# First attention of a two-block metaformer on one core: relative position terms packed per head parity, 24 products per window instead of 48, from masked queries

## The chip, the cores and the metric

The kernel runs on one core of one Trainium2 chip. The metric is the device time of one execution in microseconds (us), as the median of a few runs. TensorE is PE in the rows (its weight loads are PEld), VectorE is DVE, ScalarE is ACT, GpSimd is POOL and SyncE is SP.

## The reference, cut to what matters

Four images of 64x64 pixels and 128 channels pass through attention, a gated feed-forward layer, a second attention and a graph layer with a mixture of experts. The change is in the first attention, `_L0_conv_ref`:

```python
q = (x @ w_q).reshape(B, hh, BLOCK, ww, BLOCK, NUM_HEADS, kd)     # windows of 8x8 queries, 8 heads of 16
...
rel_w = _rel_to_abs(jnp.einsum('bghwd,dr->bghwr', pos_q, pos_emb_w))
rel_h = _rel_to_abs(jnp.einsum('bgwhd,dr->bgwhr', q_t, pos_emb_h))
return rel_h[..., :, None] + rel_w[..., None, :]
...
scores = jnp.einsum('bnhwqd,bnhwkd->bnhwqk', attn_q, key)         # 64 queries x 144 keys per window and head
attn = jax.nn.softmax(scores + pos, axis=-1)
out = jnp.einsum('bnhwqk,bnhwkv->bnhwqv', attn, value)
```

Every query has 12 numbers for the row of a key (`rel_h`) and 12 for its column (`rel_w`), and a key's position term is the sum of one of each. Each image has 64 windows, in 8 strips of 8.

## The kernel before

Each engine has its own program, written out by hand in order; semaphores tie them together, and nothing reorders them. `image(b)` runs for the four images one after the other, and the first attention (`l0conv_pe`, `l0conv_act`, `l0conv_dve`) is its first stage. Before and after the four images come long stages without it (a sort and search at the start, the graph's edges and the experts at the end).

For strip h, `queries(h)` makes the queries of all 128 channels (8 heads of 16) in the PSUM bank `top`, and ScalarE copies them window by window to QW. `relative(h,a)` multiplies them by EH (a=0, rows) or EW (a=1, columns): block diagonal weights, one 128x128 matrix for each of the 8 query positions y on that axis, 8 products of 64 moving columns in f32, which makes 16 weight loads and 16 matmul rows in the trace. Head h's 12 numbers land in its own 16 partitions. ScalarE evicts them to REST and, with VectorE (`rest`, `second`), splits them into three bf16 parts ZZ.

For a window w, `S(w)` makes the scores of 8 heads in four banks, as eight tiles of 32 rows and 64 columns of the array: row group j holds heads 2j and 2j+1, and the two column halves are the even heads (o=0) and the odd heads (o=1). Two heads share the 32 rows, so for the keys there are two copies masked by head parity (`n.PAR`), KS[0] in SB_ and KS[1] in SA_. To the 8 products with the keys, 48 products with the 0/1 matrices INDB are added in the bank: three bf16 parts, two axes, eight tiles.

TensorE's order in the loop over w, with i=w%8, is: `S(w+1)`, `weighted(w-1)` (attention times values, L392), `turn(w)` (eight transposes, L382), and one further piece: `values` (L374) for even i, for odd i `relative(h+1,0)` at i=1, `relative(h+1,1)` at i=3, `project(h-1)` at i=5 and `queries(h+2)` at i=7. VectorE's order is norm(w) (L228 and L230, normalizes the exponentials), mx(w+1) (L224, the maximum over the scores), `rest` for i=2 to 5, the copy of half the transposes (L259), and the merge of the two parities (L235, L237). ScalarE's is ex(w) (four exponentials, L303, with their sums), `turned` (L307), `queries` at i=0 (L281), `values` for odd i (L311), `relative` (L293, L295) at i=2 and 4, `second` (L298) at i=3 and 5, and `patches` (L288) at i=3. `S(w+1)` waits for ex(w), since both use the four score banks. Ahead of the loop stands a prologue: all keys (L346, ten pieces, each evicted by both ScalarE, L285, and VectorE, L215), `relative(0,0)`, `relative(0,1)`, the first values and `queries(1)`.

Of the kernel before, what the change touches and what calls it, by code (L numbers as in the profile page):

```python
# [13 lines left out]
P=128; IMGS=4; IMGTOK=4096; TILES=32; C=128  # L14

def declare_dense(nc, ctx, SA, SB):
# [4 lines left out]
    n=N()  # L21
# [51 lines left out]
    n.INDB=sb("INDB",[P,2,2,144],bf16)  # L73
# [3 lines left out]
def sync_weights(sp, n, d):  # L77
# [22 lines left out]
    for h in range(8):  # L100
        for t,nm in ((n.EH,"pos_emb_h"),(n.EW,"pos_emb_w")):
            for q in range(8):
                ld(t[16*h:16*h+16,q,16*h:16*h+12],d[nm][:,11-q:23-q])
# [5 lines left out]
def dve_prep(dve,n,iota):  # L109

    dve.wait_ge(n.w_load,n.NW)
    dve.tensor_scalar(n.PAR4[:,:],n.PAR[:,:],0.25,None,ALU.mult)
    for a,ind in enumerate((n.INDH,n.INDW)):
        for o in range(2): dve.tensor_scalar(n.INDB[:,a,o,:],ind[:,:],n.PAR[:,o:o+1],None,ALU.mult)
    dve.tensor_copy(n.DIGI[:,:],iota[:,0:16]); dve.drain()
    for r,(shift,_) in enumerate(DIGITS): dve.tensor_scalar(n.DIGS[:,r,:],n.DIGI[:,:],shift,None,ALU.logical_shift_left)
    dve.drain()
# [82 lines left out]
ROWMAJOR="p (y w x) -> p w y x"; COLMAJOR="p (x w y) -> p w y x"; WINDOWS="p (w y x) -> p w y x"  # L200
# [70 lines left out]
def l0conv_act(act,n,PSB,b,d):  # L271
# [7 lines left out]
    def queries(h):  # L279
        act.wait_ge(n.s_q,b*8+(h+1))  # L280
        act.activation(n.QW[:,h%2,:].rearrange(WINDOWS,w=8,y=8),top.rearrange(ROWMAJOR,y=8,w=8),ACT.Copy).then_inc(n.s_qc,1)  # L281
# [7 lines left out]
    def relative(h,a):  # L289
# [3 lines left out]
        act.activation(n.REST[:,:].rearrange(WINDOWS,w=8,y=8),top.rearrange((ROWMAJOR,COLMAJOR)[a],w=8,y=8),ACT.Copy).then_inc(n.s_pe,1)  # L293
# [40 lines left out]
def l0conv_pe(pe,n,PSB,ident,b):  # L334
# [12 lines left out]
    def relative(h,a):  # L347

        if a==0: pe.wait_ge(n.s_qc,b*8+(h+1))
        q=n.QW[:,h%2,:].rearrange(("c (w y x) -> c y w x","c (w y x) -> c x w y")[a],w=8,y=8)  # L350
        for y in range(8):
            last=pe.matmul(top[:,64*y:64*(y+1)],(n.EH,n.EW)[a][:,y,:],q[:,y,:,:],start=True,stop=True)  # L352
        last.then_inc(n.s_p,1)
    def S(w):
# [9 lines left out]
        for k in range(3):  # L364
            for a in range(2):
                for r,o,out in tiles: last=pe.matmul(out,n.ZZ[h%2][a][k][r,64*i:64*i+64],n.INDB[r,a,o,:],start=False,stop=(k==2 and a==1),skip_group_check=True)  # L366
# [409 lines left out]
def declare_nodes(nc,ctx,n,SA,m):  # L776
# [23 lines left out]
    n.G4=sb("G4",[P,NT,4]); n.BG=sb("BG",[P,16]); n.GM=sb("GM",[P,16]); n.BT=sb("BT",[P,16])  # L800
# [804 lines left out]
```

## Time and profile before

| | us |
|---|---|
| median of 3 runs | 7053.45 (7039.84 to 7058.35) |
| the profiled execution | 7049.08 |
| its span, first to last instruction | 7047.3 |
| TensorE matmul busy | 2995.6 (43%) |
| VectorE busy | 3414.0 (48%) |
| ScalarE busy | 1543.3 (22%) |
| GpSimd busy | 2605.7 (37%) |

The difference between the execution's time and its span is what lies around the first and the last instruction. A mean over the whole span says little here, since the stages have different limits: the four first attentions start at about 1001.6, and the last scores of the last one are made at 3277.6. Stage and step have to be looked at by themselves.

### The profile page before, as it was taken

How to read it: one execution, taken by the hardware profiler on the slowest of the kernel's cores; microseconds unless marked ns; L12 is line 12 of the kernel's file. 1: busy time of each engine (PE TensorE's matmuls, PEld its weight loads, DVE VectorE, ACT ScalarE, POOL GpSimd, SP SyncE). 2: the span in 40 equal slices, each digit the busy share in tenths (PEclk: the TensorE clock that was granted, in tenths of full speed). 3: DMA queues.
4: the chain of work that ended last, by engine and by line, in shares of the span. 5: the costliest groups of instructions: out<-in, count | busy, mean ns of one | idle time of the engine just before them, and what ended most of it. 6: DMA issues, size and time to landing. Idle time of an engine off the chain costs nothing.

```text
span 7047.3 us, 83154 instructions
## 1 busy us (share of the span) xinstructions
PE 2995.6 (43%) x31245; PEld 1791.3 (25%) x31245; DVE 3414.0 (48%) x7000; ACT 1543.3 (22%) x3959; POOL 2605.7 (37%) x2472
## 2 busy tenths in 40 slices
PE   0011149766987897788760222222222222222204
PEld 0011138424842673376220000000000000000103
DVE  9999988576857685777661111111111111111138
ACT  0000027403730463165200111111111111111100
POOL 0000000051011000100017777777777777777450
PEclk9975569866986798698755656565655555555556
DMA  2000040002000100010022222222122222222216
GB/s 82 0 0 0 0 168 4 4 18 56 4 12 1 40 3 1 13 17 3 1 33 22 34 33 33 33 33 33 28 31 33 33 29 31 33 33 33 65 46 218
DMA packets 259879, 227.73 MB, mean 32 GB/s; under 512 B 115180, under 2 KB 223128, under 8 KB 250456
## 3 DMA queue, kind: packets, MB, share of 16 engines
q0 software_dynamic: 78944, 29.28, 6.6%
q1 hardware_dynamic: 99960, 99.91, 4.6%
q10 hardware_dynamic: 80640, 93.86, 4.3%
q8 instruction: 237, 3.88, 0.2%
q14 instruction: 98, 0.80, 0.0%
HBM read 100.42 MB, written 121.39 MB: 31 GB/s over the span
## 4 chain that ended last, share of the span: by engine, by line
PE 27%; issue 20%; another core or an unknown queue 19%; DVE 19%; DVEq 7%; ACT 4%; DMA 3%; POOL 1%; ACTq 1%; SPq 0%
DVE SA_ L1325 3%; PE PSB L382 2%; PE PSB L1175 2%; DVE SA_ L1315 2%; PE PSB L686 2%; PE PSB L668 2%; PE PSB L352 2%; PE PSB L526 2%; DVEq L1406 2%; PE PSB L392 1%; PE PSB L518 1%; DVE SA_ L590 1%; DMA VPAD<-s_TNT 1%; PE PSB L366 1%
## 5 line engine op out<-in xcount | busy, mean ns | idle before, releaser
L962 POOL DMA_INDIRECT SA_<-s_T,GIX x2048 | 2166.4, 1058 | 675.7 <-issue 675.7
L1175 PE MATMUL PSB<-VPAD,EH 128*128 128x512 f32 x512 | 302.0, 754 | 1994.1 <-DMA VPAD<-s_TNT 1643.1
L907 DVE TENSOR_TENSOR XPAD<-SA_ 128x256 f32<-128x256 f32 x32 | 13.6, 425 | 1789.9 <-DMA SA_<-s_T,GIX 1789.9
L954 POOL DMA_INDIRECT s_AEXP<-fill,SIX x128 | 149.6, 1169 | 1557.3 <-DVE SA_ L587 1472.2
L858 POOL DMA_INDIRECT SA_<-s_SK,BLKI x128 | 131.5, 1028 | 1484.3 <-PE PSB L710 1389.0
L1175 PEld LDWEIGHTS PSB<-VPAD,EH 128*128 128x128 f32 x512 | 121.6, 246 | 2195.3 <-DMA VPAD<-s_TNT 1681.4
L1179 PE MATMUL PSB<-SA_,EW 128*128 128x512 f32 x512 | 345.6, 824 | 342.1 <-ACT SA_ L1160 181.0
L1429 PE MATMUL PSB<-ident,SA_ 128*128 128x128 f32 x448 | 83.1, 368 | 837.1 <-DVE SA_ L1396 575.1
L303 ACT ACTIVATE PRX<-PSB,MX 128x144 f32<-128x144 f32 x1024 | 375.2, 380 | 210.3 <-DVE MX L224 210.1
L1164 ACT ACTIVATE VPAD<-PSB,PRX 128x512 f32<-128x512 f32 x128 | 87.9, 687 | 1308.8 <-remote 969.0
L1160 ACT ACTIVATE SA_<-PSB,PRX 128x512 f32<-128x512 f32 x256 | 175.9, 687 | 770.6 <-issue 327.0
L916 DVE TENSOR_TENSOR SB_<-SA_,SB_ 128x1024 f32<-128x1024 f32 x32 | 39.2, 1225 | 562.5 <-ACT SB_ L933 313.8
L1429 PEld LDWEIGHTS PSB<-ident,SA_ 128*128 128x128 f32 x448 | 77.4, 198 | 842.5 <-DVE SA_ L1396 579.0
L382 PE MATMUL PSB<-ident,PRX 128*72 128x128 f32 x2048 | 277.4, 279 | 1.0 <-DVE PRX L230 0.5
L1325 DVE TENSOR_TENSOR SA_<-SA_ 128x2048 f32<-128x2048 f32 (+1 forms) x124 | 254.3, 2051 | 8.6 <-issue 0.4
L1179 PEld LDWEIGHTS PSB<-SA_,EW 128*128 128x128 f32 x512 | 121.1, 250 | 539.7 <-issue 322.5
L1326 DVE TENSOR_TENSOR SA_<-SA_ 128x2048 f32<-128x2048 f32 (+1 forms) x124 | 253.4, 2044 | 0.0
L587 DVE TENSOR_TENSOR SA_<-PSB,VPAD 128x512 f32<-128x512 f32 x288 | 194.5, 685 | 119.0 <-PE PSB L686 119.0
L1347 ACT ACTIVATE SA_<-PSB 128x256 f32<-128x256 f32 x112 | 42.9, 383 | 875.6 <-PE PSB L1429 873.6
L259 DVE COPY VPAD<-PSB 72x512 f32<-72x512 f32 x256 | 175.6, 686 | 106.6 <-PE PSB L382 105.2
L382 PEld LDWEIGHTS PSB<-ident,PRX 128*72 128x72 f32 x2048 | 208.2, 116 | 53.2 <-issue 30.3
L224 DVE TENSOR_REDUCE MX<-PSB 128x4 f32<-128x576 f32 x256 | 192.9, 754 | 36.4 <-PE PSB L366 35.7
(365 smaller groups left out, 7339.3 us busy)
## 6 DMA issues: line engine op xcount, KB each, us to landing
SA_<-s_T,GIX POOLq DMA_INDIRECT x2048
s_Y<-VPAD ACTq DMA_DIRECT2D x32, 1024.0 KB
s_R<-zero SPq DMA_DIRECT2D x96, 256.0 KB, 2.9
s_R<-XPAD ACTq DMA_DIRECT2D x32, 768.0 KB
SB_<-s_Y SPq DMA_DIRECT2D x16, 1024.0 KB, 5.5
SA_<-s_Y SPq DMA_DIRECT2D x16, 1024.0 KB, 6.2
s_AEXP<-zero SPq DMA_DIRECT2D x32, 256.0 KB, 3.0
SA_<-in_x SPq DMA_DIRECT2D x16, 512.0 KB
```

Source lines behind the costliest of these rows:

```text
L224: dve.tensor_reduce(n.MX[:,w%2,:],PSB[:,0:2048].rearrange("p (j x) -> p j x",j=4)[:,:,0:144],AX.X,ALU.max,negate=True).then_inc(n.s_mx,1)
L259: dve.tensor_copy(n.PTS[:,4:8,:],PSB[0:72,5*512:6*512].rearrange("p (a q) -> p a q",a=4)).then_inc(n.s_ptd,1)
L303: last=act.activation(n.PR_[:,w%2,j,:],PSB[:,j*512:j*512+144],ACT.Exp,bias=n.MX[:,w%2,j:j+1],accum_out=n.SM[:,w%2,j:j+1])
L382: last=pe.transpose(PSB[0:72,o:o+P],n.PR_[:,w%2,j,72*g:72*g+72],ident)
L587: dve.tensor_tensor(rows(to),rows(PSB[:,bank*512:(bank+1)*512]),tap(n.VD,m,TAPS[j]),ALU.mult).then_inc(n.s_p2,1)
L962: pool.indirect_dma_start(out=n.G[:,s,c,:],out_offset=None,in_=d["T"],in_offset=IOA(ap=n.GIX[s][:,c:c+1],axis=0)).then_inc(n.gath[s],16)
L1160: act.activation(n.HM2[:,m,:],PSB[:,(m%4)*512:(m%4+1)*512],ACT.Gelu,bias=n.B1M[:,m:m+1]).then_inc(n.moe_ge,1)
L1175: pe.matmul(PSB[:,(m%4)*512:(m%4+1)*512],n.WM1[:,m//2,(m%2)*P:(m%2+1)*P],n.TNC[:,s,:],start=True,stop=True).then_inc(n.moe_h,1)
L1179: for f in range(2): last=pe.matmul(PSB[:,(4+e)*512:(5+e)*512],n.WM2[:,2*e+f,:],n.HM2[:,2*e+f,:],start=(f==0),stop=(f==1))
L1325: dve.tensor_tensor(x,a,b,ALU.min)
L1326: return dve.tensor_tensor(y,a,b,ALU.max)
L1429: last=pe.transpose(PSB[:,q*P:(q+1)*P],src[:,q*P:(q+1)*P],ident)
```

## The change

In one 32-row group there are two heads with 16 rows each, and the 12 numbers of one axis fill 12 of the 16. A head needs 12 rows for each axis, so both axes of ONE head fit into the 32 rows, the row numbers in the first 16 and the column numbers in the last 16. The changed kernel makes such a packed array for the even heads (a=0) and one for the odd heads (a=1). For that the queries are also copied twice more with the other parity's heads set to zero (QM[0], QM[1]; the scale of the copy is a column of PAR), EH and EW get their 12 columns at new offsets, and each `relative(h,a)` makes 8 products with EH and 8 with EW on QM[a] and adds them up in `top`, writing each query where its window has it, so that the eviction reads in plain order. INDB becomes one matrix, and `S` has 3 x 8 products with it.

```diff
-    n.INDB=sb("INDB",[P,2,2,144],bf16)
+    n.INDB=sb("INDB",[P,144],bf16); n.G4=sb("G4",[P,128,4]); n.QM=[V[:,4352:4864],n.G4[:,:,:].rearrange("p t e -> p (t e)")]
...
-        for t,nm in ((n.EH,"pos_emb_h"),(n.EW,"pos_emb_w")):
+        for t,nm,o in ((n.EH,"pos_emb_h",h//2*32),(n.EW,"pos_emb_w",h//2*32+16)):
             for q in range(8):
-                ld(t[16*h:16*h+16,q,16*h:16*h+12],d[nm][:,11-q:23-q])
+                ld(t[16*h:16*h+16,q,o:o+12],d[nm][:,11-q:23-q])
...
-    for a,ind in enumerate((n.INDH,n.INDW)):
-        for o in range(2): dve.tensor_scalar(n.INDB[:,a,o,:],ind[:,:],n.PAR[:,o:o+1],None,ALU.mult)
+    dve.tensor_scalar(n.INDB[:,:],n.INDH[:,:],n.PAR[:,0:1],None,ALU.mult); dve.drain()
+    dve.scalar_tensor_tensor(out=n.INDB[:,:],in0=n.INDW[:,:],scalar=n.PAR[:,1:2],in1=n.INDB[:,:],op0=ALU.mult,op1=ALU.add)
...
     def queries(h):
         act.wait_ge(n.s_q,b*8+(h+1))
-        act.activation(n.QW[:,h%2,:].rearrange(WINDOWS,w=8,y=8),top.rearrange(ROWMAJOR,y=8,w=8),ACT.Copy).then_inc(n.s_qc,1)
+        act.activation(n.QW[:,h%2,:].rearrange(WINDOWS,w=8,y=8),top.rearrange(ROWMAJOR,y=8,w=8),ACT.Copy)
+        if h: act.wait_ge(n.s_p,b*16+2*h)
+        for o in range(2): last=act.activation(n.QM[o].rearrange(WINDOWS,w=8,y=8),top.rearrange(ROWMAJOR,y=8,w=8),ACT.Copy,scale=n.PAR[:,o:o+1])
+        last.then_inc(n.s_qc,1)
...
-        act.activation(n.REST[:,:].rearrange(WINDOWS,w=8,y=8),top.rearrange((ROWMAJOR,COLMAJOR)[a],w=8,y=8),ACT.Copy).then_inc(n.s_pe,1)
+        act.activation(n.REST[:,:],top,ACT.Copy).then_inc(n.s_pe,1)
...
         if a==0: pe.wait_ge(n.s_qc,b*8+(h+1))
-        q=n.QW[:,h%2,:].rearrange(("c (w y x) -> c y w x","c (w y x) -> c x w y")[a],w=8,y=8)
-        for y in range(8):
-            last=pe.matmul(top[:,64*y:64*(y+1)],(n.EH,n.EW)[a][:,y,:],q[:,y,:,:],start=True,stop=True)
+        for t,form in ((n.EH,"c (w y x) -> c y w x"),(n.EW,"c (w y x) -> c x w y")):
+            q,out=(v.rearrange(form,w=8,y=8) for v in (n.QM[a],top))
+            for i in range(8):
+                last=pe.matmul(out[:,i,:,:],t[:,i,:],q[:,i,:,:],start=(i==0 and t is n.EH),stop=(i==7 and t is n.EW),skip_group_check=True)
         last.then_inc(n.s_p,1)
...
         for k in range(3):
-            for a in range(2):
-                for r,o,out in tiles: last=pe.matmul(out,n.ZZ[h%2][a][k][r,64*i:64*i+64],n.INDB[r,a,o,:],start=False,stop=(k==2 and a==1),skip_group_check=True)
+            for r,o,out in tiles: last=pe.matmul(out,n.ZZ[h%2][o][k][r,64*i:64*i+64],n.INDB[r,:],start=False,stop=(k==2),skip_group_check=True)
```

The edit adds three lines ahead of `relative` on TensorE, so in the changed kernel L346 has become L349, L352 L356, L363 L367, L366 L369, L374 L377, L382 L385, L392 L395; on ScalarE the new copies are L283.

TensorE in the loop, from the transposes of window 1 to the scores' second half two blocks on, before (L352 is `relative`):

```order
L382 MATMUL PSB<-ident,PRX 72x128 [waits s_nrm]
L382 MATMUL PSB<-ident,PRX 72x128 x7
L352 MATMUL PSB<-QW,EH 128x64 [waits s_qc,s_vc]
L352 MATMUL PSB<-QW,EH 128x64 x7
L363 MATMUL PSB<-SB_,QW 64x144 [waits s_exp]
L363 MATMUL PSB<-SB_,QW 64x144 x3
L363 MATMUL PSB<-SA_,QW 64x144 x4
L366 MATMUL PSB<-INDB,SA_ 64x144 x48
```

The same place in the changed kernel (VPAD is where QM[0] lies):

```order
L385 MATMUL PSB<-ident,PRX 72x128 [waits s_nrm]
L385 MATMUL PSB<-ident,PRX 72x128 x7
L356 MATMUL PSB<-VPAD,EH 128x8x8 [waits s_qc,s_vc]
L356 MATMUL PSB<-VPAD,EH 128x8x8 x7
L356 MATMUL PSB<-VPAD,EW 128x64 x8
L367 MATMUL PSB<-SB_,QW 64x144 [waits s_exp]
L367 MATMUL PSB<-SB_,QW 64x144 x3
L367 MATMUL PSB<-SA_,QW 64x144 x4
L369 MATMUL PSB<-INDB,SA_ 64x144 x24
```

The block of `relative` has 16 products instead of 8, and the block of scores behind it 24 instead of 48 with INDB.

ScalarE in the loop, at the first window of a strip (L307 copies half the transposes, L303 are the exponentials), before:

```order
L307 ACTIVATE VPAD<-PSB 72x512 [waits s_tr]
L281 ACTIVATE QW<-PSB 128x512 [waits s_q]
L303 ACTIVATE PRX,SM<-PSB,MX 128x144 [waits s_mx]
L303 ACTIVATE PRX,SM<-PSB,MX 128x144 x3
L307 ACTIVATE VPAD<-PSB 72x512 [waits s_tr]
```

And in the changed kernel (G is where QM[1] lies, in the tile G4):

```order
L310 ACTIVATE VPAD<-PSB 72x512 [waits s_tr]
L281 ACTIVATE QW<-PSB 128x512 [waits s_q]
L283 ACTIVATE VPAD<-PSB,PAR 128x512 [waits s_p]
L283 ACTIVATE G<-PSB,PAR 128x512
L306 ACTIVATE PRX,SM<-PSB,MX 128x144 [waits s_mx]
L306 ACTIVATE PRX,SM<-PSB,MX 128x144 x3
```

Two copies of 128x512 stand between the copy to QW and the next exponentials.

## Rows read from the trace of the kernel before

**Rows 1.** Stretches: each engine's busy time (rows), TensorE's granted clock, DMA.

```profile
1018.00:1031.00 13.00, 10.34 (x320) 9.16 (x315) 6.83 (x14) 8.90 (x31) 0.00 (x0) 0.87 0.97 359
...
1200.00:1262.00 62.00, 55.09 (x1538) 45.87 (x1538) 49.97 (x116) 42.13 (x163) 0.00 (x0) 1.00 0.01 3
```

**Rows 2.** Timeline: the products with INDB in one strip, start and duration.

```profile
1105.75 0.68 PE L366 MATMUL PSB<-INDB,SA_ 32*64 32x144 bf16 x48
...
1109.99 0.68 PE L366 MATMUL PSB<-INDB,SA_ 32*64 32x144 bf16 x48
...
1113.40 0.68 PE L366 MATMUL PSB<-INDB,SA_ 32*64 32x144 bf16 x48
...
1117.07 0.68 PE L366 MATMUL PSB<-INDB,SA_ 32*64 32x144 bf16 x48
...
1121.30 0.68 PE L366 MATMUL PSB<-INDB,SA_ 32*64 32x144 bf16 x48
...
1124.71 0.68 PE L366 MATMUL PSB<-INDB,SA_ 32*64 32x144 bf16 x48
...
1129.11 0.68 PE L366 MATMUL PSB<-INDB,SA_ 32*64 32x144 bf16 x48
...
1132.52 0.68 PE L366 MATMUL PSB<-INDB,SA_ 32*64 32x144 bf16 x48
...
1136.16 0.68 PE L366 MATMUL PSB<-INDB,SA_ 32*64 32x144 bf16 x48
```

**Rows 3.** Timeline of the step with `relative(h+1,0)`.

```profile
1117.09 0.76 DVE L230 TENSOR_TENSOR PRX<-PRX,RSM 128x576 f32<-128x576 f32 x1
...
1118.27 1.07 PE L382 MATMUL PSB<-ident,PRX 128*72 128x128 f32 x8
...
1119.17 1.90 PE L352 MATMUL PSB<-QW,EH 128*128 128x64 f32 x16
```

**Rows 4.** Timeline of the step with `relative(h+1,1)`.

```profile
1125.02 0.76 DVE L230 TENSOR_TENSOR PRX<-PRX,RSM 128x576 f32<-128x576 f32 x1
...
1125.91 0.81 PEld L382 LDWEIGHTS PSB<-ident,PRX 128*72 128x72 f32 x8 [0.20 <-DVE PRX L230]
...
1126.82 2.06 PE L352 MATMUL PSB<-QW,EW 128*128 128x64 f32 x16
```

**Rows 5.** Timeline of the step behind `relative(h+1,0)`.

```profile
1122.01 0.76 DVE L224 TENSOR_REDUCE MX<-PSB 128x4 f32<-128x576 f32 x1 [0.48 <-PE PSB L366]
...
1124.41 0.15 PEld L363 LDWEIGHTS PSB<-SB_,QW 32*64 32x64 f32 x4 [0.18 <-ACT PRX L303]
```

**Rows 6.** Waits in image 0's window loop, 1018 to 1261: total, times, longest.

```profile
PEld PSB L363 <- ACT PRX L303: 17.1, 37, 2.8
...
DVE MX L224 <- PE PSB L366: 9.6, 18, 1.7
```

**Rows 7.** The line of `relative` in the whole run: ns, min/median/max.

```profile
L352 PE MATMUL PSB<-QW,EH x512: 219/275/324, 1005.0 to 3232.6; 128*128 128x64 f32 x171
...
L352 PE MATMUL PSB<-QW,EW x512: 276/298/303, 1008.4 to 3240.5; 128*128 128x64 f32 x171
```

**Rows 8.** Timeline of the prologue, where copies have a scale from PAR.

```profile
1004.34 1.75 ACT L285 ACTIVATE SB_<-PSB,PAR 128x476 f32<-128x476 f32 x3
...
1011.27 2.26 ACT L285 ACTIVATE SB_<-PSB,PAR 128x476 f32<-128x476 f32 x3 [1.43 <-PE PSB L346]
...
1018.53 1.28 ACT L303 ACT_TABLE_LOAD   x1
```

**Rows 9.** Timeline of the step with the copy of the queries.

```profile
1113.41 0.60 ACT L281 ACTIVATE QW<-PSB 128x512 f32<-128x512 f32 x1
...
1115.16 0.38 ACT L303 ACTIVATE PRX<-PSB,MX 128x144 f32<-128x144 f32 x1 [1.15 <-DVE MX L224]
```

**Rows 10.** Timeline of the first window after the prologue.

```profile
1021.97 0.97 PE L366 MATMUL PSB<-INDB,SA_ 32*64 32x144 bf16 x48
...
1022.88 1.92 PE L382 MATMUL PSB<-ident,PRX 128*72 128x128 f32 x8
```

More of the change, by code:

```diff
@@ L199, in kbank @@
     return PSB[:,KB[c%6]*512:KB[c%6]*512+hi-lo]
-ROWMAJOR="p (y w x) -> p w y x"; COLMAJOR="p (x w y) -> p w y x"; WINDOWS="p (w y x) -> p w y x"
+ROWMAJOR="p (y w x) -> p w y x"; WINDOWS="p (w y x) -> p w y x"
 def l0conv_first_dve(dve,n,b):
@@ L799, in declare_nodes @@
     n.fe_rdy, n.fe_g, n.fo_e, n.fo_x, n.fo_rdy, n.fo_st = [sem(s) for s in ("fe_rdy", "fe_g", "fo_e", "fo_x", "fo_rdy", "fo_st",)]
-    n.G4=sb("G4",[P,NT,4]); n.BG=sb("BG",[P,16]); n.GM=sb("GM",[P,16]); n.BT=sb("BT",[P,16])
+    n.BG=sb("BG",[P,16]); n.GM=sb("GM",[P,16]); n.BT=sb("BT",[P,16])
     A=n.HTL[:,:,:,:].rearrange("p a b c -> p (a b c)")
```

## The prediction

> **What bounds the kernel now.** I first ask where the changed code runs. It runs only in the first attention of the four images, so I read that stage by itself. The windows view [rows 1] shows TensorE's matmuls busy in 55.09 of 62 us at the end of image 0's attention, at the full granted clock. No engine has much slack there, so I went on to the waits and then to single steps.
>
> I call step i the time from the scores issued in iteration i of the window loop to those issued in iteration i+1. The starts of the products with INDB give all eight steps of a strip [rows 2]: step 6 takes 4.24 us (1105.75 to 1109.99), step 7 3.41, step 0 3.67, step 1 4.23, step 2 3.41, step 3 4.40, step 4 3.41, step 5 3.64. That makes 30.41 us, and the other strips and images repeat it. The reader is to see that steps are unequal: the two dearest with one kind of work are those with `relative`, 1 and 3. They tell which chain ends last in each:
>
> - Steps 1 and 3 are bound by TensorE. Transposes start at 1118.27, `relative` at 1119.17 and lasts 1.90, and the scores follow at once [rows 2, 3]. In step 3, 1125.91, 1126.82 and 2.06 say the same [rows 4].
> - Steps 2 and 4, behind them, are bound by a round: scores, maximum, exponentials, next scores. The maximum (L224) waited 0.48 us for the products (L366), took 0.76, and TensorE then waited for the exponentials until 1124.41 [rows 5].
> - Steps 7, 0, 5 and 6 are bound by VectorE and ScalarE. In image 0 the maximum waited for the products only 18 times in 64 windows, 9.6 us together [rows 6]; in the others the normalization ahead of it on VectorE ended as late as the products. In step 6 VectorE's residual also stands between.
>
> **The change part by part.**
>
> *24 products fewer per window.* 48 take 0.68 us at the full clock [rows 2], so 14 ns each, and 24 should take 0.34 less. (The Trainium skill, "TensorE: Matmul & The Clock Gate", Part 3, says that matmuls in different tiles start about 4 ns apart. By that, 24 fewer would save only 0.10 us, and the time would be some 27 us above the sum below; the rows have 14 ns between starts, so I go by them.) What 0.34 us is worth differs by step:
>
> - Steps 2 and 4: all of it, -0.34 each. The round behind it does not change.
> - Step 1: -0.34. The transposes start at 1118.27 because scores and `weighted` precede them. The normalization ends at 1117.85 [rows 3], so they can start 0.34 earlier.
> - Step 3: only about -0.10. The normalization ends at 1125.78 and the transposes start at 1125.91 [rows 4]; they wait for VectorE already.
> - Step 7: -0.07, as the normalization then sets the maximum. Steps 0, 5, 6: nothing, covered by the exponentials' and VectorE's work. If that cover were gone, each could give up to 0.34.
>
> *Eight products more per `relative`.* A block of 16 rows is 15 starts and one matmul. EH: 1.90 us [rows 3] less one matmul of 0.275 [rows 7] is 0.108 per start, so 1.73 per block of 16; EW: 2.06 [rows 4] less 0.298 [rows 7] is 0.117, so 1.88. Every block now holds both: block (h+1,0) grows by 1.88, and block (h+1,1) by 1.73. The blocks stand where TensorE is the bound and nothing on another engine runs longer, so all of it is paid: step 1 +1.88, step 3 +1.73. The trace has no matmul that adds up at a stride into PSUM. From below, a product could cost nothing more than its start; from above I take the transposes, eight products in 1.07 us [rows 3], 0.134 per start and so 4.3 us for a block of both instead of 3.61; as the nearest row is `relative` itself, I take 3.61: the reads are those of before and only the writes are new.
>
> *Two masked copies of the queries on ScalarE.* One such copy with its scale from PAR comes every 0.58 us (three in 1.75 [rows 8]). In step 0 the copy to QW starts at 1113.41, and ScalarE then waits 1.15 us for the maximum until 1115.16 [rows 9]. Two copies of 0.60 need 1.20, so 0.05 is late, which cancels what step 0 could have gained from earlier products: 0. Behind them on ScalarE are the exponentials, and for these TensorE waits; if that gap of 1.15 were not there, the copies would cost up to 1.2 us in 24 steps (six strips in each of four images), 29 us. The values block, which waits for the copies (s_qc), has until the transposes end and is not later. The new wait on s_p is for a `relative` four windows back: free.
>
> Sum for a strip that prepares another: step 1 -0.34+1.88=+1.54, step 2 -0.34, step 3 -0.10+1.73=+1.63, step 4 -0.34, step 7 -0.07, so **+2.42 us**. There are 7 such strips in each of 4 images: 28 x 2.42 = +68. The eighth strip has no `relative`: seven steps of about -0.15 (the gain split between the two chains, my choice between 0 and 0.34), 4 x -1.05 = -4.
>
> *Prologue.* Both blocks stand on TensorE's path to the keys: ScalarE waits 1.43 us for L346 until 1011.27 [rows 8]. The blocks grow by 1.88 and 1.73, and ScalarE's first waits for them, so +3.6. After the first scores ScalarE makes two more copies ahead of the table load at 1018.53 and the first exponentials: +1.2. The load and those exponentials have no cover. 4 x 4.8 = +19.
>
> The eviction to REST, the splits and VectorE's loop keep their number and size: 0. INDB is built once: 0. The DMAs of EH and EW keep their number.
>
> Sum: 68 - 4 + 19 = +83. The profiled execution took 7049.1 us, 4 below the median of the runs shown, so 7132; I forecast **7133 us**. After the stage, the images' other stages run one behind the other on the same three engines, and nothing in them could absorb a shift.
>
> **The rivals.**
>
> - *The clock falls.* In the first window after the prologue the granted clock is 0.87 on the mean, 48 products took 0.97 instead of 0.68 and the transposes 1.92 instead of 1.07 [rows 1, 10], after TensorE had waited for the table load and the first exponentials. The stretch mixes the clock's two levels, 1.2 and 2.4 GHz. The longer blocks of short products could count as little work. If the clock fell after each of the 56 blocks in the loop, one window would pay half of 0.29 on its 24 products and 0.85 on the transposes, 1.0 us, and I add 0.4 for the pieces that I have no pair of rows for: 56 x 1.4 = +78, so 7211. (The Trainium skill, same page, Part 1, says that activity releases the throttle.) Against it: in the last 62 us of the stage, with the same blocks at its start and less other work than elsewhere behind them, the clock stays 1.00 [rows 1]. 7%.
> - *The scores don't get shorter by half.* If a window's products are held by something other than their number rounds of eight tiles with a long end, say, the gains shrink, to 30% if as little as 0.10 us is saved in a window: 28 x (0.34+0.34+0.34+0.10+0.07=1.19) x 0.7 is 23 us, with 3 of the eighth strips': 7159. (That is the Trainium skill's 4 ns, above.) Against it: the 14 ns are the same whenever the clock is full. 6%.
> - *Faster.* It decides what an added group of eight products costs where it stands. If TensorE had slack of that size in steps 1 and 3, only the gains would remain: 28 x -1.19 = -33, -4, and in the prologue the +1.2 of the copies, 4 x 1.2 = +5: 7017. The sign turns where a group costs less than 0.59 us in the loop (1.19 / 2) instead of 1.8. For it: TensorE waits for exponentials 37 times, 17.1 us in image 0 [rows 6]. Against it: those waits are in other steps, none ahead of a score block behind `relative`. 4%.
> - *Half of both:* the blocks take less than their sum, or steps 0, 5, 6 gain up to 0.3 after all, and the total is within 0.3% of nothing. 4%.
>
> **How the numbers follow.** The forecast's own bounds: below, steps 0, 5 and 6 gain 0.3 each (28 x 0.9 = 25) and half of the prologue's growth is hidden (10): 7098. Above, 4.3 us for a block of both: 64 blocks x 0.69 = +44, so 7177. I give 79% to the forecast with its bounds. With the second rival inside, the range 7095 to 7175 holds 85%. A change of 0.3% is 21 us, about what a measurement of this kernel can tell from none. Slower: 79+7+6 = 92%, less 2 for what I haven't seen; same 5%; faster 5%.
>
> **What would show it.** In the changed trace: 24 products in 0.34 us; `relative` as 32 rows in about 3.8 us from the first to the last end; steps 1 and 3 near 5.8 and 6.0 us; steps 2 and 4 near 3.07; steps 0, 5, 6 as before; the strip near 32.8 instead of 30.41; the copy of queries followed by exponentials with almost no wait on ScalarE; the first exponentials of an image some 4.8 us later after the layer norm; the clock 1.00 in the stage. It is wrong if the 32 rows take far from 3.6 us, if the clock sinks, or if the other steps move by more than 0.1.

## The result, and the profile after

| us | before | after |
|---|---|---|
| median of 4 runs each | 7048.49 (7039.84 to 7058.35) | 7152.18 (7126.79 to 7159.58) |
| ratio after/before, 95% interval | | 1.014 [1.0111, 1.017] |
| the profiled execution | 7049.08 | 7126.79 |
| its span | 7047.3 | 7125.0 |

The changed kernel is 104 us slower; 7133 was forecast, with 7095 to 7175 as the range. Its profiled execution happens to be the fastest of its four. The page of the profile, of the changed kernel, has these lines on the engines and on the queue that brings instructions:

```profile
span 7125.0 us, 72977 instructions
...
PE 3059.0 (43%) x26125; PEld 1870.7 (26%) x26125; DVE 3407.0 (48%) x6998; ACT 1578.6 (22%) x4023; POOL 2603.8 (37%) x2472
...
q8 instruction: 197, 3.23, 0.2%
```

The page of the kernel before has 31245 matmul rows. 5120 fewer are left, and yet TensorE is busier: 24 short rows left each of 256 windows, and 16 long ones (8 products) came to each of 64 blocks of `relative`. The timeline of TensorE over one strip, the changed kernel, answers to [rows 2 to 4]:

```profile
1187.35 0.48 PE L369 MATMUL PSB<-INDB,SA_ 32*64 32x144 bf16 x24
...
1191.48 0.48 PE L369 MATMUL PSB<-INDB,SA_ 32*64 32x144 bf16 x24
...
1194.78 0.48 PE L369 MATMUL PSB<-INDB,SA_ 32*64 32x144 bf16 x24
...
1198.36 0.48 PE L369 MATMUL PSB<-INDB,SA_ 32*64 32x144 bf16 x24
1200.27 1.90 PE L356 MATMUL PSB<-VPAD,EH 128*128 128x64 f32 x16
1202.01 2.08 PE L356 MATMUL PSB<-VPAD,EW 128*128 128x64 f32 x16
...
1204.32 0.48 PE L369 MATMUL PSB<-INDB,SA_ 32*64 32x144 bf16 x24
...
1207.53 0.48 PE L369 MATMUL PSB<-INDB,SA_ 32*64 32x144 bf16 x24
...
1213.57 0.48 PE L369 MATMUL PSB<-INDB,SA_ 32*64 32x144 bf16 x24
...
1216.78 0.48 PE L369 MATMUL PSB<-INDB,SA_ 32*64 32x144 bf16 x24
...
1220.42 0.48 PE L369 MATMUL PSB<-INDB,SA_ 32*64 32x144 bf16 x24
```

The differences of the starts are the steps 6, 7, 0, 1, 2, 3, 4, 5 in this order. Beside them, those of [rows 2]:

| step | 6 | 7 | 0 | 1 | 2 | 3 | 4 | 5 | strip |
|---|---|---|---|---|---|---|---|---|---|
| before | 4.24 | 3.41 | 3.67 | 4.23 | 3.41 | 4.40 | 3.41 | 3.64 | 30.41 |
| after | 4.13 | 3.30 | 3.58 | 5.96 | 3.21 | 6.04 | 3.21 | 3.64 | 33.07 |
| difference | -0.11 | -0.11 | -0.09 | +1.73 | -0.20 | +1.64 | -0.20 | 0 | +2.66 |
| forecast | 0 | -0.07 | 0 | +1.54 | -0.34 | +1.63 | -0.34 | 0 | +2.42 |

The two steps with `relative` carry the loss, and each other step gives back at most 0.20. (The median of each step over the 24 strips in the middle of the images is within 0.02 us of this strip's in the changed kernel.) The two rows of L356 begin 1.74 us apart and end together 3.82 after the first start: 16 products with their weight loads, where [rows 3] had 8 in 1.90.

To see where in an image the time went, I cut each image's first attention by the starts of its rows: from the first product with the queries' weights to the first one with INDB (the prologue), and from there to the last one with INDB (the loop).

| us, images 0 to 3 | prologue | loop |
|---|---|---|
| before | 16.5, 17.7, 16.5, 16.5 | 239.5, 237.3, 238.7, 237.2 |
| after | 20.1, 27.1, 26.5, 20.5 | 257.9, 257.4, 258.3, 257.4 |
| difference | 3.6, 9.4, 10.0, 4.0 | 18.4, 20.1, 19.6, 20.2 |

The loops give +78 and the prologues +27, +105 together. The spans differ by only 78. The missing 27 us lie in the second attention, whose code is not touched: from its first to its last matmul it took 9, 14 and 9 us less in images 0, 1 and 3 and 2 more in image 2, 30 less together; the other stretches give some 2 us back. The profiled execution lies 25 us below the median. The stage by itself agrees with the medians.

The prologue of image 1 is the place that I had not foreseen. The timeline of the changed kernel there, ScalarE and TensorE:

```profile
1726.74 0.60 ACT L281 ACTIVATE QW<-PSB 128x512 f32<-128x512 f32 x1 [5.33 <-DMA s_ADT<-VPAD]
...
1728.54 2.29 PE L356 MATMUL PSB<-VPAD,EH 128*128 128x64 f32 x16 [3.55 <-ACT G L283]
...
1730.62 3.62 PE L356 MATMUL PSB<-VPAD,EW 128*128 128x64 f32 x16
...
1734.05 3.24 PE L349 MATMUL PSB<-XPAD,WK 128*128 128x476 f32 x4
```

Windows of the changed kernel over this prologue (columns: length, then busy time of PE, PEld, DVE, ACT and POOL with their rows, granted clock, DMA share, GB/s):

```profile
1721.00:1749.00 28.00, 22.40 (x136) 15.51 (x136) 9.20 (x14) 13.54 (x24) 0.00 (x0) 0.88 0.17 4
```

The same two views of the kernel before:

```profile
1708.80 0.60 ACT L281 ACTIVATE QW<-PSB 128x512 f32<-128x512 f32 x1 [3.86 <-DMA s_ADT<-VPAD]
...
1709.45 2.00 PE L352 MATMUL PSB<-QW,EH 128*128 128x64 f32 x16 [0.93 <-ACT QW L281]
```

```profile
1705.00:1723.00 18.00, 15.48 (x111) 9.45 (x114) 9.02 (x14) 11.59 (x20) 0.00 (x0) 1.00 0.17 5
```

ScalarE stands at the head of the stage behind a wait for the store of the previous image's last results (`t_st`, DMA s_ADT<-VPAD), and only then copies the queries. Then, in the changed kernel, the two masked copies follow. TensorE makes six matmuls with the keys' weights (L349) ahead and then has nothing: 3.55 us instead of 0.93. Behind that gap its clock is at the lower of its two levels, 1.2 GHz, for a while: the EW half of the block takes 3.62 us instead of 2.08, and the granted clock of the window is 0.88 on the mean instead of 1.00. How long the store is waited for differs from run to run (below), but not what TensorE has to do meanwhile.

### The profile page after: what moved, and what is told of

Read it like the earlier page. It is cut to its first block, busy times and chain, and to the rows that moved or that the text cites. A ratio compares the mean times of both kernels' runs of the same rounds, so it can differ in the third digit from the quotient of the medians.

```text
span 7125.0 us, 72977 instructions
## 1 busy us (share of the span) xinstructions
PE 3059.0 (43%) x26125; PEld 1870.7 (26%) x26125; DVE 3407.0 (48%) x6998; ACT 1578.6 (22%) x4023; POOL 2603.8 (37%) x2472
## 4 chain that ended last, share of the span: by engine, by line
PE 25%; another core or an unknown queue 20%; DVE 19%; issue 18%; DVEq 8%; ACT 5%; DMA 4%; POOL 1%; ACTq 1%; SPq 0%
PE PSB L356 3%; DVE SA_ L1328 3%; PE PSB L1178 2%; DVE SA_ L1318 2%; PE PSB L385 2%; PE PSB L689 2%; DMA VPAD<-s_TNT 2%; PE PSB L529 2%; DVE SA_ L593 2%; DVEq L1409 2%; PE PSB L671 2%; ACT PRX L306 1%; PE PSB L521 1%; DVEq L592 1%
## 5 line engine op out<-in xcount | busy, mean ns | idle before, releaser
L385 PE MATMUL PSB<-ident,PRX 128*72 128x128 f32 x2048 | 279.9, 281 | 1.6 <-DVE PRX L230 0.9
L385 PEld LDWEIGHTS PSB<-ident,PRX 128*72 128x72 f32 x2048 | 209.7, 117 | 59.0 <-DVE PRX L230 34.2
```

Source lines behind the costliest of these rows:

```text
L385: last=pe.transpose(PSB[0:72,o:o+P],n.PR_[:,w%2,j,72*g:72*g+72],ident)
```

## The experiments

The runs below were made on four chips. On two of them the kernel before takes 7046 and 7051 us, on the other two 6732 and 6740: there the part behind the last first attention is shorter (3457 us with 24 products alone, on such a chip, against 3770 in the profile of the kernel before). Each ratio is with the kernel before on the same chip, and across the chips I compare differences in microseconds.

### One axis of 24 products alone

The kernel before, with the products of the row axis (a=0) left out of the scores, so that 24 are left in a window. No `relative` is changed.

```diff
-            for a in range(2):
-                for r,o,out in tiles: last=pe.matmul(out,n.ZZ[h%2][a][k][r,64*i:64*i+64],n.INDB[r,a,o,:],start=False,stop=(k==2 and a==1),skip_group_check=True)
+            for r,o,out in tiles: last=pe.matmul(out,n.ZZ[h%2][1][k][r,64*i:64*i+64],n.INDB[r,1,o,:],start=False,stop=(k==2),skip_group_check=True)
```

> The kernel before with the half of the INDB products left out that belongs to the row axis (a=0), so 24 instead of 48 in a window; relative, queries and all else as before (the scores lack one position term). Theory A (only the windows in which TensorE's products end last pay): the changed kernel's steps show -0.20 us in steps 1, 2 and 4, about -0.1 in steps 6, 7 and 0, none in 3 and 5, so about -0.9 us per strip, -25 to -30 us in all, 7048 to about 7020. Rival B (every window pays what the products lose, 0.20 us, 256 times): -51 us, 6997. Rival C (the forecast's 0.34 us per window where it counts): -38 us.

Measured: 6701.13 against 6731.59, 0.9955 [0.9937, 0.9972], 30 us less. Four rows of its timeline, the scores at which steps 1, 2 and 3 begin and step 3 ends:

```profile
1113.35 0.48 PE L365 MATMUL PSB<-INDB,SA_ 32*64 32x144 bf16 x24
...
1117.54 0.48 PE L365 MATMUL PSB<-INDB,SA_ 32*64 32x144 bf16 x24
...
1120.75 0.48 PE L365 MATMUL PSB<-INDB,SA_ 32*64 32x144 bf16 x24
...
1125.02 0.48 PE L365 MATMUL PSB<-INDB,SA_ 32*64 32x144 bf16 x24
```

The three steps take 4.19, 3.21 and 4.27 where [rows 2] have 4.23, 3.41 and 4.40; the group itself lasts 0.48 instead of 0.68. Step 1 of this strip is an exception: its median over the 24 middle strips is 4.03, so -0.20 like step 2. The loops of the four images (230.3, 229.9, 230.7, 230.8) are 31 us shorter together, where my own terms (28 by 1.19, and 4) make 37. So half of the products is worth 0.20 us where a window is bound by them, and not 0.34. The prologues, whose code is that of before, took 16.5, 25.5, 20.7 and 16.5; why those of images 1 and 2 are long is taken up below.

### 16 products in `relative` alone

The kernel before, with each product of `relative` issued twice.

```diff
-        for y in range(8):
-            last=pe.matmul(top[:,64*y:64*(y+1)],(n.EH,n.EW)[a][:,y,:],q[:,y,:,:],start=True,stop=True)
+        for k in range(2):
+            for y in range(8): last=pe.matmul(top[:,64*y:64*(y+1)],(n.EH,n.EW)[a][:,y,:],q[:,y,:,:],start=True,stop=True)
```

> The kernel before with relative's 8 products issued twice over (same weights again, same result), so 16 in a block, and 48 products per window as before. Theory A: 64 x 1.8 = +115 us, about 7163, and no change in the other steps. Rival (part of the block's growth is covered by other engines' work): +60 us or less. The sum of this run, of the 24 products alone and of the masked copies should give the change's +104 us.

Measured: 6848.77 against 6731.59, 1.0175 [1.0149, 1.02], +117. In the timeline of this kernel the blocks are 32 rows long:

```profile
1107.01 3.97 PE L352 MATMUL PSB<-QW,EW 128*128 128x64 f32 x32
...
1131.69 3.68 PE L352 MATMUL PSB<-QW,EH 128*128 128x64 f32 x32
```

3.68 is 1.78 more than the 1.90 of [rows 3], and 3.97 is 1.91 more than the 2.06 of [rows 4]. The loops grow by 25.1, 25.7, 24.8 and 25.7 us, 101 together, which is 28 strips by the 3.61 of the forecast. The prologues grow by 3.7, 10.5, 11.3 and 3.7: those of images 1 and 2 by far more than 3.6 here too, without one masked copy. In image 1 ScalarE waited 5.95 us for the store and TensorE 3.01 us for the queries; the granted clock of the prologue is 0.82 on the mean (a row of the timeline, and one of the windows view with columns as above):

```profile
1716.61 7.09 PE L352 MATMUL PSB<-QW,EH 128*128 128x64 f32 x32 [3.01 <-ACT QW L281]
...
1710.00:1739.00 29.00, 24.33 (x160) 17.26 (x160) 9.21 (x14) 12.26 (x22) 0.00 (x0) 0.82 0.20 4
```

The parts nearly add up. In the medians, 24 products alone and 16 alone give -30 and +117, +87 together, against +98 to +104, and the intervals of the two are together wider than the gap. In the loops they give -31 and +101, +70, against +78; the masked copies in the first windows add some 5 (next two runs).

### Eight products in `relative`, the rest as changed

The changed kernel, where a block makes only EH's products (a=0) or only EW's (a=1); the other axis' term is left out of each.

```diff
-        for t,form in ((n.EH,"c (w y x) -> c y w x"),(n.EW,"c (w y x) -> c x w y")):
+        for t,form in (((n.EH,"c (w y x) -> c y w x"),(n.EW,"c (w y x) -> c x w y"))[a],):
...
-                last=pe.matmul(out[:,i,:,:],t[:,i,:],q[:,i,:,:],start=(i==0 and t is n.EH),stop=(i==7 and t is n.EW),skip_group_check=True)
+                last=pe.matmul(out[:,i,:,:],t[:,i,:],q[:,i,:,:],start=(i==0),stop=(i==7),skip_group_check=True)
```

> The changed kernel with relative cut back to 8 products (EH alone for a=0, EW alone for a=1, still on the masked queries; each head gets one of its two position terms). Theory A (the added 8 products per relative are paid in full on TensorE's path): 64 x 1.8 = -115 us against the changed kernel, about 7037, slightly faster than before. Rival (half of the loss comes from the masked copies and from the new waits): no less than 7090.

Measured: 6702.84 against 6731.59, 0.9963 [0.9948, 0.9979], 29 us less than before. That is within 2 us of the kernel with 24 products alone, so everything else in the change (masked copies, the new writes) is close to free in the medians, and the doubled blocks turn -29 into the +98 to +104 measured for the changed kernel. Its loops take 231.7, 231.2, 231.7 and 231.6, between 0.8 and 1.4 us more than with 24 products alone. Its prologues take 16.5, 25.3, 24.7 and 18.2: those of images 1 and 2 are long without doubled blocks too.

### No masked copies

The changed kernel without the two masked copies; `relative` reads QW, so the parities are mixed.

```diff
...
-        if h: act.wait_ge(n.s_p,b*16+2*h)
-        for o in range(2): last=act.activation(n.QM[o].rearrange(WINDOWS,w=8,y=8),top.rearrange(ROWMAJOR,y=8,w=8),ACT.Copy,scale=n.PAR[:,o:o+1])
...
-            q,out=(v.rearrange(form,w=8,y=8) for v in (n.QM[a],top))
+            q,out=(v.rearrange(form,w=8,y=8) for v in (n.QW[:,h%2,:],top))
```

> The changed kernel without the two masked copies of the queries; relative reads QW (the two parities' numbers are then mixed). Theory A: the copies cost nothing in the window loop, 1.2 us twice in each of four prologues, and another 6 to 7 us in the prologues of images 1 and 2, where TensorE now waits longer for the copies, its clock falls and the relative block runs at 1.2 GHz: together -10 to -24 us against the changed kernel, 7128 to 7142. Rival (the copies hold up the exponentials in step 0 as well): another -10 or more, below 7125.

Measured: 6807.83 against 6731.59, 1.0116 [1.0093, 1.014], +76, so 22 to 28 us below the changed kernel's +98 to +104 across the chips, at the edge of the 10 to 24 that were expected. The loops (257.2, 255.7, 256.7, 255.8) are 5.6 us shorter together than with the copies, nearly all of it in the first windows of an image; step 0 is the same. The prologues of images 1 and 2 fall from 27.1 and 26.5 to 20.9 and 20.7. In the timeline of this kernel, image 1:

```profile
1709.44 2.00 PE L353 MATMUL PSB<-QW,EH 128*128 128x64 f32 x16 [0.55 <-ACT QW L281]
```

TensorE waited for 0.55 us and its blocks ran at the full clock. But the store's wait was shorter in this execution, 3.49 us, so this run alone does not tell how much of the 12 us belongs to the copies and how much to the store.

### The changed kernel again

> The changed kernel once more, unchanged, beside the others on their chip. Theory A: the first attention takes 22 us more per image than before in each execution, and about 7 more in the prologues of images 1 and 2 where ScalarE waits for the store of the image before; the second attention, shorter by 9, 7 and 4 us in the first profile of the changed kernel, is as long as before on the mean. So the ratio is near 1.014 again. Rival (the changed kernel makes later stages faster): the second attention is again 154 to 168 us in all four images.

Measured: 7143.21 against 7045.58, 1.0134 [1.0117, 1.0151], +98. Prologues 20.2, 26.7, 26.6 and 20.1, loops 257.7, 257.0, 258.3 and 257.6: the stage repeats within 1 us. The second attention, from its first to its last matmul, is 9 us shorter in all than in the kernel before (248.0, 237.5, 226.0 and 226.4 against 249.6, 237.4, 224.0 and 235.5), and not 30 as in the first profile. So the changed kernel does not make it faster in each execution.

### The wait for the store moved behind the queries

The changed kernel; ScalarE waits for the store only after it has copied the first queries.

```diff
-    if b: act.wait_ge(n.t_st,b*32)
...
-    queries(0); patches(0)
+    queries(0)
+    if b: act.wait_ge(n.t_st,b*32)
+    patches(0)
```

> The changed kernel, complete, with ScalarE's wait for the store of the image before (t_st) moved from ahead of queries(0) to ahead of patches(0), the first that writes over what is stored. Theory A (in the prologues of images 1 and 2 ScalarE's wait of 4 to 5 us keeps the queries' three copies from TensorE, which then stands idle and falls to the lower clock): those prologues last 20 to 21 us instead of 27, -12 to -14 us in all against the changed kernel. Rival (the lower clock comes from the longer relative blocks themselves): the prologues keep 24 us or more.

Measured: 6830.49 against 6739.59, 1.0134 [1.0115, 1.0152], +91. In the timeline of image 1 ScalarE's wait is now behind the copies, and in the windows view (columns as above) the clock is full:

```profile
1725.26 1.16 ACT L290 ACTIVATE VPAD<-XPAD 128x1152 f32<-128x1152 f32 x1 [2.94 <-DMA s_ADT<-VPAD]
```

```profile
1719.00:1741.00 22.00, 19.27 (x136) 13.07 (x136) 9.31 (x15) 13.68 (x24) 0.00 (x0) 1.00 0.28 5
```

The prologues of images 1 and 2 take 20.8 and 20.2, some 6 us less each, with all masked copies in place (that of image 3 took 21.8, with a granted clock of 0.57 over 4 us at its head). So the excess came from queries that the store's wait made late, from TensorE's idle time and from the lower clock behind it. It was not the copies by themselves: the kernel with 16 products alone has the same excess and no copy. In the total, 7 to 13 us less than the changed kernel is within the uncertainty; only the stage shows it.

### The same move in the kernel before

The same edit, made to the kernel before.

> The kernel before with that wait moved alone, complete. Theory A: its prologues of images 1 to 3 lose 1.2 us when the store is as early as in the profile shown, and up to 9 when it is late by 7 us as in e1; so 0 to -10 us, not above 0.15%.

Measured: 6739.15 against 6739.59, 0.9998 [0.9984, 1.0011]: nothing. ScalarE waits for the store as before, 8.4 us in 2 waits, now ahead of the keys' evictions, and the prologues of images 1 and 2 took 22.4 and 19.0, more than the 17.7 and 16.5 of the kernel before. The timeline of image 1:

```profile
1694.43 3.67 PE L353 MATMUL PSB<-QW,EW 128*128 128x64 f32 x16 [2.57 <-ACT REST L292]
```

TensorE now waits for the eviction of the first block, which ScalarE makes behind the store's wait, and the second block takes 3.67 us instead of 2.06. With blocks half as long as in the changed kernel, the early queries give TensorE too little to bridge the wait; that the length of the blocks decides it was not tested by itself.

### Packed terms in 32x32 tiles, without masks

If the doubled blocks are the loss, make them cheaper. A head pair's queries need only their own 32 rows and make only 32 columns, so the block diagonal product splits into four tiles of 32x32 of the array, side by side. Parity moves into the weights (EHT, EWT: the other parity's rows are zero), and the masked copies go.

```diff
...
-        for t,form in ((n.EH,"c (w y x) -> c y w x"),(n.EW,"c (w y x) -> c x w y")):
-            q,out=(v.rearrange(form,w=8,y=8) for v in (n.QM[a],top))
+        for t,form in ((n.EHT,"c (w y x) -> c y w x"),(n.EWT,"c (w y x) -> c x w y")):
+            q,out=(v.rearrange(form,w=8,y=8) for v in (n.QW[:,h%2,:],top))
...
+                for r in (slice(32*j,32*j+32) for j in range(4)):
+                    last=pe.matmul(out[r,i,:,:],t[r,a,i,:],q[r,i,:,:],start=(i==0 and t is n.EHT),stop=(i==7 and t is n.EWT),skip_group_check=True)
```

> The changed kernel, complete, with two things other: the head parity is put into the position weights (two small sets, one for even and one for odd heads) so that there are no masked copies of the queries, and relative's products are made in tiles of 32 rows and 32 columns of the array, four for each position, 64 instead of 16 in a block. Theory A (the block's time is 128-column weight loads in a row, and tiles of different rows and columns overlap as the INDB products do, 10 to 14 ns from start to start): 128 rows in 1.3 to 1.8 us instead of 3.6, steps 1 and 3 near 3.9 us, about -4.2 us per strip, so -118 us in the loops and -25 to -40 in the prologues against the changed kernel, some 40 to 50 us below the kernel before (0.6 to 0.7%). Rival (small f32 products in tiles do not overlap, 30 to 60 ns each): 4 to 8 us a block, slower than the changed kernel.

Measured: 7086.15 against 7045.58, 1.0063 [1.0047, 1.0079], +41: much better than the changed kernel, and a miss of some 85 us. The timeline shows where:

```profile
1102.50 1.10 PE L355 MATMUL PSB<-QW,EH 32*32 32x64 f32 x64
1103.42 2.06 PE L355 MATMUL PSB<-QW,EW 32*32 32x64 f32 x64
```

EH's half fell from 1.90 to 1.10, where 0.65 to 0.9 was expected, and EW's stayed at 2.06. The rows view of this line in the whole run says that one EW matmul lasts 292 ns where an EH one lasts 214:

```profile
L355 PE MATMUL PSB<-QW,EH x4096: 214/214/239, 1005.7 to 3275.0; 32*32 32x64 f32 x196
...
L355 PE MATMUL PSB<-QW,EW x4096: 270/292/293, 1006.6 to 3276.8; 32*32 32x64 f32 x196
```

Both have 64 columns. EH reads and writes the queries in runs of eight side by side, EW reads and writes them at a stride of 8 elements. One of the two accesses is the suspect.

### Tiles in the kernel before

The kernel before with its 8 products split into the same four tiles, and nothing packed.

```diff
...
-            last=pe.matmul(top[:,64*y:64*(y+1)],(n.EH,n.EW)[a][:,y,:],q[:,y,:,:],start=True,stop=True)
+            for r in (slice(32*j,32*j+32) for j in range(4)):
+                last=pe.matmul(top[r,64*y:64*(y+1)],(n.EHT,n.EWT)[a][r,y,:],q[r,y,:,:],start=True,stop=True,skip_group_check=True)
```

> The kernel before, complete, with relative's products alone in 32x32 tiles, 32 instead of 8 in a block, and 48 products per window as before. Theory A: 64 rows in 0.65 to 0.9 us instead of 1.8, steps 1 and 3 fall to what ScalarE and VectorE leave, about 3.65 us, so -1.3 us per strip, -36 us, and -8 us in the prologues: 0.6% below the kernel before. Rival as for the other: blocks of 2 to 4 us, slower than before.

Measured: 7030.96 against 7045.58, 0.9982 [0.9971, 0.9994], 15 us less. Step 1 takes 3.52 instead of 4.23, step 2 3.55 instead of 3.41 and step 3 4.49 instead of 4.40; 28 strips by -0.48 is -13. The loops of the profiled execution are only 7 us shorter together, and some 44 had been expected in all. The EW block gained nothing: it writes without a stride here and takes 2.06 again, so the write is not the cause.

### A copy in column order

The packed tiles, with a second copy of the queries on ScalarE in the order in which EW reads them.

```diff
...
+        if h: act.wait_ge(n.s_p,b*16+2*h)
+        act.activation(n.QM[1].rearrange("p (x w y) -> p x w y",x=8,w=8),top.rearrange("p (y w x) -> p x w y",y=8,w=8),ACT.Copy).then_inc(n.s_qc,1)
...
+            q=n.QW[:,h%2,:].rearrange(form,w=8,y=8) if t is n.EHT else n.QM[1].rearrange("c (x w y) -> c x w y",x=8,w=8)
```

> The kernel of t1 (packed, parity in the weights, 32x32 tiles), complete, with one more copy of the queries on ScalarE in column order, from which the EW products read 64 neighbouring columns instead of columns at a stride of 8. Theory A (a tiled f32 product is bound by the columns it streams, and a stride of 8 in the moving operand halves that rate: 64 EH rows at 14 ns, 64 EW rows at about 30 ns): a block falls from 2.8 to about 1.8 us, steps 1 and 3 from 5.2 to 4.2, so -64 us against t1, plus 4 for the copy in the prologues: about 20 us below the kernel before (0.3%). Rival (the strided write to PSUM is what costs): no change against t1.

Measured: 6757.64 against 6739.59, 1.0036 [1.0021, 1.005], +18, which is 23 us below the packed tiles and not the 64 expected. The rows view says that the stride was the cause:

```profile
L358 PE MATMUL PSB<-G,EW x4096: 211/214/238, 1005.0 to 3262.8; 32*32 32x64 f32 x196
...
  issue: 43.0, 112
```

An EW matmul lasts 214 ns like an EH one, though it still writes at the stride. But the second line, idle time ahead of this line's rows put down to nothing but issuing, is 43.0 us; it was 20.2 with the packed tiles and is 2.7 in the changed kernel. In the timeline it stands inside a block:

```profile
1101.51 1.06 PE L358 MATMUL PSB<-G,EW 32*32 32x64 f32 x61
...
1103.21 0.30 PE L358 MATMUL PSB<-G,EW 32*32 32x64 f32 x3 [0.65 <-issue]
```

61 matmuls at a stretch, then 0.65 us of nothing, then the last three. This is taken up below.

### Both edits on the packed form

The column copy and the moved wait together.

> t3 with that wait moved as well, complete: the version that should beat both kernels, -5 to -10 us against t3, so 25 to 30 us below the kernel before (0.4%).

Measured: 6748.49 against 6739.59, 1.0017 [1.0006, 1.0027], +9: 9 us less than with the column copy alone, which the intervals of the two don't tell from nothing, and some 35 above what was expected. The packed form with the cheapest blocks that I found is not faster than the kernel before.

### Tiles and column copy in the kernel before

48 products and one axis per block, as before, with tiles, the column copy and the moved wait.

```diff
...
-        q=n.QW[:,h%2,:].rearrange(("c (w y x) -> c y w x","c (w y x) -> c x w y")[a],w=8,y=8)
+        q=n.QC.rearrange("c (x w y) -> c x w y",x=8,w=8) if a else n.QW[:,h%2,:].rearrange("c (w y x) -> c y w x",w=8,y=8)
```

> The kernel before with 48 products and relative in 32x32 tiles as in t2, the EW queries read from a copy in column order as in t3, and the wait for the store moved as in t4; complete. Theory A (the EW tiles of t2 are bound by reading at a stride; half as many instructions in a block as in t3, so that their supply keeps up): the EW block falls from about 1.9 to 0.9 us, step 3 from 4.5 to about 3.7, -20 us against t2 and about 30 us (0.4%) below the kernel before. Rival (instructions arrive too slowly here as well, or the copy on ScalarE costs in every strip): within 0.2% of the kernel before, and TensorE idle for 'issue' as long as in t3 (43 us in the line of relative).

Measured: 7026.05 against 7050.64, 0.9962 [0.9947, 0.9977], 25 us less: it beats both kernels. The idle time for issuing is 18.5 us. Of the strip in its timeline:

```profile
1116.23 0.68 PE L372 MATMUL PSB<-INDB,SA_ 32*64 32x144 bf16 x48
...
1119.76 0.68 PE L372 MATMUL PSB<-INDB,SA_ 32*64 32x144 bf16 x48
...
1123.31 0.68 PE L372 MATMUL PSB<-INDB,SA_ 32*64 32x144 bf16 x48
1125.60 1.10 PE L358 MATMUL PSB<-VPAD,EW 32*32 32x64 f32 x64
1127.27 0.68 PE L372 MATMUL PSB<-INDB,SA_ 32*64 32x144 bf16 x48
```

Step 1 takes 3.53, step 2 3.55 and step 3 3.96, 1.00 less than in [rows 2] together. In the whole profiled execution less comes of it: the loops (236.7, 235.4, 233.9, 233.9) are 13 us shorter together and the prologues 4. The EW block shrinks by 0.96 but step 3 by only 0.44, since another chain ends last then.

## Why the prediction was right

The direction, the place and the mechanism were right; the size was 19 us short. Step by step:

- **Eight products more per `relative`.** Right. Forecast +1.88 and +1.73 a block; with this part alone the loops grew by 101 us, as 28 by 3.61 gives. The bound from above (4.3 us for both) did not come near: 3.82 from first start to last end. It divided the extent of eight transposes, 1.07, by 8, with the last whole one in it; 279 ns of that taken off, the same rows give 3.8. The write at a stride that adds up in PSUM costs nothing visible, since 1.90 and 2.08 are the 1.90 and 2.06 of [rows 3, 4].
- **24 products fewer.** Right in kind, and the term that was mis-sized. I divided 0.68 by 48. But that extent holds one whole matmul behind the last start, which doesn't halve. One lasts 225 ns at the median in the kernel before:

```profile
L366 PE MATMUL PSB<-INDB,SA_ x12288: 217/225/323, 1018.1 to 3277.6; 32*64 32x144 bf16 x199
```

  With it taken off, 47 starts of some 10 ns are left, and 24 products fewer would have been 0.23 us. 24 take 0.48, so 0.20 is saved and not 0.34: 8 ns for each product left out, and not 14. Steps 2 and 4 gained 0.20 each instead of 0.34, and step 1 came out at +1.73 instead of +1.54. Against that, steps 6, 7 and 0 gained about 0.10 each, where I had put 0, -0.07 and 0, so the cover there was thinner than I took it to be. The strip came to +2.66 instead of +2.42, 28 by 0.24 is 7 us. By that alone, steps 1, 2 and 4 came out 0.42 above the forecast; the gains of 6, 7 and 0 gave back 0.24 of it, so the strip is nearer the forecast than its terms are. (I had made the right correction for the blocks of `relative`, 15 starts and one matmul, and not for these. The Trainium skill, "TensorE: Matmul & The Clock Gate", Part 3, has 4 ns between starts; the rows have 8, between its figure and mine.)
- **Masked copies in the loop.** Right. The timeline of ScalarE in step 0, the changed kernel:

```profile
1194.79 0.60 ACT L281 ACTIVATE QW<-PSB 128x512 f32<-128x512 f32 x1
1195.27 0.69 ACT L283 ACTIVATE VPAD<-PSB,PAR 128x512 f32<-128x512 f32 x1
...
1195.84 0.70 ACT L283 ACTIVATE G<-PSB,PAR 128x512 f32<-128x512 f32 x1
1196.46 0.38 ACT L306 ACTIVATE PRX<-PSB,MX 128x144 f32<-128x144 f32 x1
```

  The exponentials follow the copies without a wait, where [rows 9] had a gap of 1.15, and the step takes 3.58.
- **Prologue.** Right for images 0 and 3: 20.1 and 20.5 instead of 16.5, where +3.6 was forecast. The copies ahead of the first exponentials also cost what they should: in image 0 the first window takes 5.03 instead of 3.86 (+1.2). The second took 4.55 instead of 4.01, 0.5 that I had not counted. TensorE had been idle for 4.01 us in the first instead of 2.66. The granted clock from 1026 to 1036 is 0.66 on the mean, and in the second window the products for the values (L377) took 1.91 us instead of 1.17 (L374). Over the four images the two windows cost 7.8 us more, where +4.8 was forecast. Wrong for images 1 and 2, +9.4 and +10.0. There the step that failed is that I read one prologue, image 0's, and multiplied by 4. Image 0 has no store ahead of it. In images 1 and 2 ScalarE comes late to the queries, the copies make it later, and TensorE's clock falls, so this is the rival "the clock falls" at another place than where I put it. The timelines of seven kernels (us, images 1 and 2):

| | ScalarE waits for the store | then TensorE for the queries | prologue |
|---|---|---|---|
| before | 3.86, 2.27 | 0.93, 0 | 17.7, 16.5 |
| 24 products alone | 7.91, 5.24 | 4.98, 2.30 | 25.5, 20.7 |
| 16 products alone | 5.95, 5.74 | 3.01, 2.80 | 28.3, 27.8 |
| no masked copies | 3.49, 3.24 | 0.55, 0.30 | 20.9, 20.7 |
| eight products, the rest as changed | 6.70, 5.71 | 4.92, 3.93 | 25.3, 24.7 |
| changed | 5.33, 4.70 | 3.55, 2.92 | 27.1, 26.5 |
| changed, again | 4.87, 4.80 | 3.09, 3.02 | 26.7, 26.6 |

  TensorE waits 2.94 us less than ScalarE without masked copies, and 1.78 less with them, so the copies lengthen its idle time by 1.16 us. With the waits of the changed kernel and no copies it would still be 2.4 and 1.8 (an estimate from these differences); one of 2.30 cost 4.2 us with the code of before. So of these 13 us a good part goes with the length of the store's wait, which the kernel before can meet too, and the change's own share stays open. Whether the change makes that wait longer was not tested. Moving the wait, with the copies kept, took 6 us off each of the two.
- **The sum.** Loops: forecast +69 (68, less 4, and 4 by 1.2 for the first windows), measured +78. Prologues: forecast +14, measured +27. Together +105 in the stage and +98 to +104 in the medians, where the forecast had +83. That the median fell inside the range owes something to its width: 13 of the 22 us missing in the stage come from a cost that no bound of the range was built from.
- **The rivals.** Behind the first windows of an image the granted clock of the loop is 1.00 (from 1036 to 1282 in image 0 and from 1758 to 2006 in image 1): no fall behind the long blocks. The second rival, short gains, is partly true: 0.20 of 0.34 where the products bind, for a reason that it names (a long end), and 0.95 of 1.19 us in a strip (3.61 for the blocks, less the 2.66 measured). Its 30% is not. Faster is excluded: a group of eight costs about 1.8 us, three times the 0.59 from which the sign turns.

## What to carry to other kernels

The extent of a group of short matmuls is starts plus one whole matmul; take that one off before halving. Packing that saves cheap products (8 ns each, 24 in every window) can be bought too dearly with wide ones (220 ns each, even if there are only 16 more of these in a strip): put the price of both beside each other, in the steps where they end last. And read the prologue of every image, not that of the first, for what the previous one leaves to wait for.

## What the runs showed of the hardware that I had not expected

- **A strided read costs where the product is small.** 64 f32 columns read at a stride of 8 elements take 292 ns instead of 214 in a 32x32 tile, and a block of 64 rows takes 2.06 us instead of 1.10. The write to PSUM at the same stride costs nothing that shows: 214 ns with it (column copy on the packed form) and without it (column copy in the kernel before). Under a 128x128 weight load the same stride hardly shows: 2.06 for EW and 1.90 for EH, 16 rows.
- **Perhaps TensorE runs out of instructions.** What follows is argued from counts, and no run tested it. From 24 products alone to tiles and column copy, the instruction queue goes from 189 to 261 packets and TensorE's matmuls from 25100 to 34316: 9216 matmuls, as many loads, for 72 packets, so 256 instructions a packet. (From the kernel before to 24 products alone it is 6145 matmuls for 48 packets, 256 again.) A block of the packed tiles is 128 matmuls and 128 loads, one packet, in about 1.9 us. That is where the idle time for "issue" is found: 43.0 us in all with the column copy on the packed form, 18.5 with half as many rows in a block, 2.7 in the changed kernel. It would explain why the column copy on the packed form missed its forecast by 41 us, while the one in the kernel before came within 5 of its own. Whether the supply or something else stops the issue stays open.
